# Message-passing kernel on 100,000 nodes: places of the search as rows, index loads cut in pieces, dense units moved, scatter turns refined

## What is computed

```python
x = normal(100000, 128)                       # nodes
src = randint(25000); dst = sort(100000 * uniform(25000)**2)   # edges, sorted by dst
# layer 0: edge messages, maximum over the edges of one destination
xc = x[dst];  feat = concat([xc, x[src] - xc])
m  = relu(feat @ W1 + b1) @ W2 + b2
a  = segment_max(m, dst);  a[no edge] = 0
x1 = layernorm(x + a)
# layer 1: sum of the sources' rows, then two products, with a residual
h  = x1 + segment_sum(x1[src], dst)
h  = relu(h @ V1 + c1) @ V2 + c2
out = layernorm(x1 + x1 @ Wres + bres + h)
```

## Time and profile before

| what | value |
|---|---|
| time, median of 3 runs | 1157.18 us (1156.98 to 1157.43) |
| profiled execution, its own time | 1157.41 us |
| its span | 1155.6 us, so 1.81 us lie around it |
| busy in the span | PE 1083.7 us (94%), DVE 939.1 (81%), ACT 896.5 (78%), POOL 764.7 (66%) |
| stages, from start times in the trace | head to 57.5, S to about 278, A to about 588, dense units to 605.8, B to about 925, C to 1136.3, scatters to 1155.6 |

### The profile page before, as it was taken

How to read it: one execution, slowest core, us unless ns; L and a number is a source line. 1 busy time by engine, 2 the same in 40 slices (tenths; PEclk the granted TensorE clock), 3 DMA queues, 4 the chain that set the end, 5 groups by cost and what they waited for, 6 DMA issues and landing times.

```text
span 1155.6 us, 27075 instructions
## 1 busy us (share of the span) xinstructions
PE 1083.7 (94%) x7463; PEld 836.6 (72%) x7463; DVE 939.1 (81%) x3648; ACT 896.5 (78%) x3876; POOL 764.7 (66%) x798
## 2 busy tenths in 40 slices
PE   4699999999999999999979999999999999999992
PEld 3477777776666666666658888888888888888882
DVE  5588988987888888888858778777777799999981
ACT  1578888887888888888867888888888877777772
POOL 6777777777777766662037777777777777777006
PEclk9899999999999999999989999999999999999997
DMA  4578778885787887776566666666655566666532
GB/s 135 173 225 233 238 238 242 240 235 169 196 223 216 219 231 204 216 216 181 169 196 199 211 204 191 210 206 191 206 173 180 182 217 220 215 217 221 180 135 82
DMA packets 172193, 232.04 MB, mean 201 GB/s; under 512 B 25508, under 2 KB 90641, under 8 KB 172044
## 3 DMA queue, kind: packets, MB, share of 16 engines
q1 hardware_dynamic: 145372, 180.84, 49.9%
q0 software_dynamic: 25088, 48.94, 16.8%
q10 hardware_dynamic: 1584, 0.53, 0.2%
HBM read 129.48 MB, written 102.96 MB: 201 GB/s over the span
## 4 chain that ended last, share of the span: by engine, by line
PE 54%; POOL 26%; issue 10%; DVE 7%; DMA 1%; ACT 1%; DVEq 0%; SPq 0%; POOLq 0%; ACTq 0%
POOL edge_rows L507 16%; PE psY L1100 10%; PE psY L1099 10%; PE psH L1108 9%; PE psT L1092 5%; POOL xd_early L507 4%; PE psE L1092 4%; POOL src_bc L507 4%; PE psE L1100 4%; PE psE L1099 4%; PE psE L1251 4%; PE psE L1215 3%; DVE shared L733 3%; DVE shared L744 2%; POOL out L511 1%
## 5 line engine op out<-in xcount | busy, mean ns | idle before, releaser
L1099 PE MATMUL psY<-wc,hT 128*128 128x128 f32 x1568 | 305.9, 277 | 2.6 <-ACT o_rows L948 2.2
L1100 PE MATMUL psY<-wcr,xT 128*128 128x128 f32 x1568 | 305.3, 277 | 0.0
L511 POOL DMA_INDIRECT out<-edge_rows,idx x196 | 195.0, 995 | 116.7 <-DMA out<-o_rows 57.5
L507 POOL DMA_INDIRECT edge_rows<-x1e_table,idx x196 | 189.0, 965 | 124.6 <-DMA x1e_table<-shared 65.1
L923 ACT ACTIVATE junk<-psY 128x128 f32<-128x128 f32 x784 | 209.5, 300 | 50.9 <-PE psY L1100 50.9
L1099 PEld LDWEIGHTS psY<-wc,hT 128*128 128x128 f32 x1568 | 240.7, 194 | 3.9 <-issue 3.9
L1100 PEld LDWEIGHTS psY<-wcr,xT 128*128 128x128 f32 x1568 | 240.4, 194 | 0.0
L507 POOL DMA_INDIRECT edge_rows<-in_x,idx x196 | 190.2, 970 | 66.0 <-issue 59.5
L585 DVE TENSOR_SCALAR x<-x_in,mv,rs 128x128 f32<-128x128 f32 x784 | 220.5, 359 | 0.5
L1108 PE MATMUL psH<-xT,wc 128*128 128x512 f32 x392 | 205.5, 606 | 16.0 <-DVE deltas L664 10.2
L579 DVE BATCH_NORM_STATS2 bn_a<-x_in 128x6 f32<-128x128 f32 x784 | 164.6, 271 | 19.6 <-DMA x_in<-in_x 19.5
(11 more groups left out here) (125 smaller groups left out, 1996.3 us busy)
## 6 DMA issues: line engine op xcount, KB each, us to landing
x_in<-in_x SPq DMA_DIRECT2D x196, 256.0 KB
out<-o_rows SPq DMA_DIRECT2D x196, 256.0 KB
src_bc<-src_dram SPq DMA_DIRECT2D x49, 256.0 KB, 4.9
mask<-mask_dram SPq DMA_DIRECT2D x98, 128.0 KB
x1eT_spill<-x1eT SPq DMA_DIRECT2D x49, 256.0 KB, 2.5
x1e_table<-edge_rows SPq DMA_DIRECT2D x49, 256.0 KB, 3.3
x1e_table<-shared SPq DMA_DIRECT2D x49, 256.0 KB, 3.7
x1eT<-x1eT_spill SPq DMA_DIRECT2D x49, 256.0 KB, 3.1
```

The source lines that it names most:

```text
L507: nc.gpsimd.indirect_dma_start(to, None, table, bass.IndirectOffsetOnAxis(idx[:, what, t:t + 1], 0)).then_inc(landed[n % FLIGHT], 16)
L511: nc.gpsimd.indirect_dma_start(table, bass.IndirectOffsetOnAxis(idx[:, SCAT, t:t + 1], 0), frm, None, bounds_check=limit, oob_is_err=False ...
L1099: t_.matmul(to[:, cut(t)], h[:, cut(t)], wc2[:, :], start=t == 0, stop=False, skip_group_check=True)
L1100: last = t_.matmul(to[:, cut(t)], xt[:, cut(t)], wcr[:, :], start=False, stop=t == TILES - 1, skip_group_check=True)
```

## The change

1. `place` writes its results as rows. One stationary window of 128 columns out of `place_w` is zero except for two columns, at 2g and 2g+1. Three products with the 512 columns of `match` and `steps` as the moving operand add the group's pair of rows to `psE[2]`, where all 49 groups accumulate. `keep_places` is gone from the steps. `lead_a` copies the bank, PE transposes it in four tiles, and DVE copies the pairs out.
2. Index loads of 67 rows become 64 and 3, those of 127 rows 112 and 15, also the copy of `parts`. One more small load reads the last destinations of three tiles. In all 8 more DMAs from SP, all in the head.
3. Head: the scaling of unit 1 on DVE moves ahead of a wait for PE, and PE waits for the second weights only before it first uses them.
4. Steps 49, 50 and 51 of A now each end with a whole dense unit. Four dense units still follow. B starts at unit 79 in place of 76, and C has 3 units fewer.
5. Scatter turns: groups 45, 46, 47 have turns of their own, and so have the first three tiles of group 48; only its last tile waits for all stores. The last unit stores only the 160 rows that are its own, without the wait.

```diff
+    A_LAST = FIRST_A + A_UNITS
+    BORDER = A_LAST + STEPS - GROUPS
+    EVEN = 16
+    PART_ROWS = (FULL - P) // EVEN * EVEN
+    PAIR_AT = 2 * GROUPS - 2
+    WINDOW = PAIR_AT + P
...
-            for s in range(STEPS):
+            for s in range(GROUPS):
                 step_a(s, FIRST_A + s // A_STEPS if s // A_STEPS < A_UNITS else None, s % A_STEPS)
+            for s in range(GROUPS, STEPS):
+                step_a(s, None, 0)
+                dense(A_LAST + s - GROUPS)
...
-                    if n == UNITS - 1:
-                        sp.wait_ge(stored[(n - 1) % SLOTS], 16 * ((n - 1) // SLOTS + 1))
-                    sp.dma_start(rows_of(out, n), o_rows[:, n % SLOTS, :]).then_inc(stored[n % SLOTS], 16)
+                    own = slice((UNITS * ROWS - N) // TILES if n == UNITS - 1 else 0, P)
+                    sp.dma_start(rows_of(out, n)[own, :], o_rows[own, n % SLOTS, :]).then_inc(stored[n % SLOTS], 16)
...
-                sp.dma_start(parts_above[1:P, :, :], parts[0:P - 1, :, :]).then_inc(s_above, 16)
+                sp.dma_start(parts_above[EVEN:P, :, :], parts[EVEN - 1:P - 1, :, :]).then_inc(s_above, 16)
+                sp.dma_start(parts_above[1:EVEN, :, :], parts[0:EVEN - 1, :, :]).then_inc(s_above, 16)
...
+            def load_second(to, a, done):
+                rows = a.rearrange("(j p) -> j p", p=P)
+                sp.dma_start(to[0:PART_ROWS, :], rows[0:PART_ROWS, :]).then_inc(done, 16)
+                sp.dma_start(to[PART_ROWS:FULL - P, :], rows[PART_ROWS:FULL - P, :]).then_inc(done, 16)
...
+            for g in range(WHOLE):
                 pool.wait_ge(res_done, g + 1)
+                if g % SLOTS == 0 or g > LATE:
+                    await_stores(count)
...
+            for g in range(WHOLE, GROUPS):
+                pool.wait_ge(res_done, g + 1)
+                for t in range(TILES):
+                    await_stores(count if t < WHOLE_TILES else 16 * BODIES)
+                    if t + 1 < WHOLE_TILES:
+                        count = stores_needed(WHOLE + t + 1)
                     scatter(out, edge_rows[:, cut(g * TILES + t)], g * TILES + t, scatter_number(g) + t)
...
             def lead_a():
-                dve.wait_ge(places_done, GROUPS)
+                dve.wait_ge(pos_done, GROUPS)
+                v.tensor_copy(place_rows, psE[2][:, :]).then_inc(rows_kept, 1)
+                copy_xs(0)
+                dve.wait_ge(rows_turned, 1)
+                v.tensor_copy(places.rearrange("p (g t) c -> p t g c", t=TILES),
+                              tiles(psE[3][:, :])[:, :, 0:2 * GROUPS]
+                              .rearrange("p t (g c) -> p t g c", c=2)).then_inc(places_done, 1)
...
-                    for t in range(TILES):
-                        to = psE[2 + q][:, 2 * t:2 * t + 2]
-                        t_.matmul(to, match[:, q, cut(t)], place_w[:, 0:2], start=True, stop=False,
-                                  skip_group_check=True)
-                        t_.matmul(to, steps[:, r, 0, cut(t)], place_w[:, 2:4], start=False, stop=False,
-                                  skip_group_check=True)
-                        last = t_.matmul(to, steps[:, r, 1, cut(t)], place_w[:, 2:4], start=False, stop=True,
-                                         skip_group_check=True)
+                    t_.matmul(psE[2][:, :], place_w[:, 0, window], match[:, q, :], start=g == 0, stop=False,
+                              skip_group_check=True)
+                    for h in range(2):
+                        last = t_.matmul(psE[2][:, :], place_w[:, 1, window], steps[:, r, h, :], start=False,
+                                         stop=g == GROUPS - 1 and h == 1, skip_group_check=True)
...
             def lead_a():
                 pe.wait_ge(match_done, GROUPS)
-                pe.wait_ge(places_done, GROUPS)
                 transpose_in(0)
+                pe.wait_ge(rows_kept, 1)
+                transpose4(psE[3], place_rows, rows_turned)
...
                 if n > 0:
-                    dense(n)
+                    first_half(n)
+                if n == 2:
+                    pe.wait_ge(s_dv, WEIGHT_STEPS)
+                second_product(n - 2)
...
             link(v.tensor_tensor(wtmp[:, 0, :], raw[:, RES, :], ident[:, :], ALU.add))
+            norm1_scale(1)
             dve.wait_ge(s_pe, 2)
...
-            pe.wait_ge(s_dv, WEIGHT_STEPS)
             walk(head, dense, lead_s, step_s, lead_a, step_a, lead_b, step_b)
```

More of the change, by code:

```diff
@@ L28, in gnn_program @@
     BODIES = UNITS // SLOTS
-    assert UNITS == BODIES * SLOTS and N % 32 == 0
+    assert UNITS == BODIES * SLOTS and N % 32 == 0 and (UNITS * ROWS - N) % TILES == 0
     GROUPS = -(-E // ROWS)
@@ L98, in gnn_program @@
         assert WHOLE % SLOTS == 0
-        last_dst = sb("last_dst", [1, WHOLE], I32)
-        stores_16 = sb("stores_16", [1, WHOLE], I32)
+        WHOLE_TILES = FULL - WHOLE * TILES
+        LATE = WHOLE - SLOTS
+        last_dst = sb("last_dst", [1, WHOLE + WHOLE_TILES], I32)
+        stores_16 = sb("stores_16", [1, WHOLE + WHOLE_TILES], I32)
         x_in = sb("x_in", [P, SLOTS, ROWS])
@@ L176, in gnn_program @@
         pos_done = sem("pos_done")
+        rows_kept = sem("place_rows_kept")
+        rows_turned = sem("place_rows_turned")
         places_done = sem("places_done")
@@ L539, in _, with stores_needed, await_stores, last_group_of @@
                     gather(edge_rows[:, cut(g * TILES + t)], x1e_table, PLACE, g * TILES + t, z_number(g) + t)
-            def stores_needed(g):
-                top = g + SLOTS - 1
-                earlier = pool.value_load(stores_16[0:1, top:top + 1], min_val=0, max_val=16 * LAST)
+            def stores_needed(at):
+                earlier = pool.value_load(stores_16[0:1, at:at + 1], min_val=0, max_val=16 * LAST)
                 return pool.snap(earlier + 16)
+            def await_stores(count):
+                for k in range(SLOTS):
+                    pool.wait_ge(stored[k], count)
+                pool.nop().then_inc(s_turn, 1)
+            def last_group_of(g):
+                return g + SLOTS - 1 if g < LATE else g
             pool.wait_ge(s_dv, SETUP_STEPS)
-            count = stores_needed(0)
-            for g in range(GROUPS):
-                r = g % SLOTS
+            count = stores_needed(last_group_of(0))
+            for g in range(WHOLE):
                 pool.wait_ge(res_done, g + 1)
-                if g < WHOLE and r == 0:
-                    for k in range(SLOTS):
-                        pool.wait_ge(stored[k], count)
-                    pool.nop().then_inc(s_turn, 1)
-                elif g == WHOLE:
-                    for k in range(SLOTS):
-                        pool.wait_ge(stored[k], 16 * BODIES)
-                for t in range(TILES):
-                    if t == TILES - 1 and r == SLOTS - 1 and g + 1 < WHOLE:
-                        count = stores_needed(g + 1)
+                if g % SLOTS == 0 or g > LATE:
+                    await_stores(count)
+                for t in range(TILES):
+                    if t == TILES - 1 and (g % SLOTS == SLOTS - 1 or g >= LATE):
+                        count = stores_needed(last_group_of(g + 1) if g + 1 < WHOLE else WHOLE)
+                    scatter(out, edge_rows[:, cut(g * TILES + t)], g * TILES + t, scatter_number(g) + t)
+            for g in range(WHOLE, GROUPS):
[4 more added lines that the diff above has]
+                        count = stores_needed(WHOLE + t + 1)
                     scatter(out, edge_rows[:, cut(g * TILES + t)], g * TILES + t, scatter_number(g) + t)
@@ L626, in dense @@
             def dense(n):
-                norm1_scale(n + 1)
+                if n > 0:
+                    norm1_scale(n + 1)
                 norm1_var(n + 2)
@@ L652, in find @@
                                     ALU.is_equal).then_inc(match_done, 1)
-            def keep_places(g):
-                if is_group(g):
-                    dve.wait_ge(pos_done, g + 1)
-                    v.tensor_copy(places[:, g * TILES:(g + 1) * TILES, :],
-                                  psE[2 + g % 2][:, 0:2 * TILES]
-                                  .rearrange("p (n c) -> p n c", c=2)).then_inc(places_done, 1)
             def lead_s():
-                dve.wait_ge(s_above, 32)
+                dve.wait_ge(s_above, 48)
                 v.tensor_tensor(deltas[:, :, :, :].rearrange("p a h j -> p a (h j)"), parts, parts_above,
```

46 lines of the change are left out of this document (26 added, 20 removed).

## The result

The changed kernel takes **1144.44 us** (median of 4 runs, 1143.42 to 1146.15) against 1157.31 (1156.98 to 1157.93) for the one before: ratio 0.989, interval 0.9873 to 0.9907. The prediction was 1144.5. The profiled execution of the changed kernel is the longest of its four: 1146.15 us, span 1144.0. Its ledger therefore closes at -11.6 us of span, where the medians differ by 12.9.

What follows compares the result with a forecast made beforehand. PE was taken to bound S and C, with holes in the head and at A's end, and POOL scattering after PE's last product. Terms +16.9, +0.3, -14.5, -4.4, -11.2 sum to -12.9: 1157.41 to 1144.5 us, range 1138.5 to 1152.0.

Steps and rivals of the forecast that it cites:

- places in S: Search stage S: three wide products at 0.645 us replace twelve at 0.30; step 4.25 us grows by 0.345, +16.9 us.
- `lead_a`: Start of A: added copies and four transposes mostly fit PE's 0.77 us wait for ACT; +0.3 us, between 0 and 2.5.
- head: Before S: smaller row counts shorten SP's issues and PE's 10.2 us hole goes; net -14.5 us, between -17.5 and -9.
- units at the end of A: A's end to B: three more dense units fill PE's idle time, paced by ACT; -4.4 us, between -1 and -9.
- turns and tail: Span's end: finer turns let POOL scatter earlier, span ending at 1144.4; -11.2 us, between -10.5 and -12.
- what was named as late next: End of head: the first sources' broadcast, sent near 41, needing 4.9 us; PE waits 1 us, then 2.2 for a `finish`.
- B's first step near 613: Sign for the units at A's end: B's first step starts near 613 us.
- The counts 12, 5 and 3: Last twenty scatters: twelve go early, five at 1128.4, three wait for the last store.
- (d): Rival in S: wide products overlap down to the narrow ones' price, S stays as before; 1127.6 us, chance 0.03.
- (e): Rival in the head: number of DMAs binds SP, not rows; hole stays, head +2.3, 1161.3 us; chance 0.05.
- (b): Rival in the head: another transfer takes the hole's place, 6 to 9 us remain; head -7, 1152 us, chance 0.17.
- (c): Rival: full cover at A's end and the head at its best, 5 to 6 us more; 1138.5 us, chance 0.11.

Runs made afterwards that it cites:

- run 1: The changed kernel measured again with no edit: 1144.77 us, ratio 0.9902 to the kernel before.
- run 2: The changed kernel with the twelve narrow products, the copies in each step and the old `lead_a` back: 1128.34 us, ratio 0.9754 to the kernel before.
- run 3: The kernel before with the wide products and new `lead_a`, plus the extra load of last destinations and the last short store without its wait: 1173.3 us, ratio 1.0126.
- run 4: The changed kernel with index loads of 67 and 127 rows whole again, the copy of `parts` still cut: 1150.92 us, ratio 0.9948 to the kernel before.
- run 5: The changed kernel with the copy of `parts` cut into 113 and 14 rows instead of 112 and 15: 1151.28 us, ratio 0.9953 to the kernel before.
- run 6: The changed kernel with the head's old order (unit 1 scaled after DVE's waits, PE waiting for all weights first): 1145.94 us, ratio 0.9889 to the kernel before.
- run 8: The changed kernel with the three dense units moved from the end of A back to C: 1149.67 us, ratio 0.9944 to the kernel before.
- run 9: The changed kernel with the old scatter turns, one for four groups and one for the last group: 1155.49 us, ratio 0.9986 to the kernel before.
- run 10: The changed kernel with the last group's counts read before its first wait: 1144.49 us, ratio 0.9897 to the kernel before.

## Why the prediction was right

The ledger, from starts in the traces. "After" is the execution whose own time is 1146.15, "again" is run 1. For S the predicted 0.345 times 49 is kept, as 38 steps give 0.346 each.

| term | predicted | after | again |
|---|---|---|---|
| places in S | +16.9 | +16.9 | +16.9 |
| `lead_a` | +0.3 | -0.2 | -0.2 |
| head | -14.5 | -13.2 | -14.5 |
| units at the end of A | -4.4 | -4.8 | -5.0 |
| turns and tail | -11.2 | -10.4 | -10.9 |
| sum, with A +0.1 | -12.9 | -11.6 | -13.6 |

- **Places.** Right: 0.65 us for three, a step of 4.59. The value was chosen by the distance between starts of the same form; that was the choice that mattered. By the Trainium skill's 131 ns the step would be an estimated 4.34, and the forecast 12 us too low. Runs 2 and 3 price the part at 16.4 and 15.1 to 15.7, net of `lead_a` and of when S began.
- **`lead_a`.** Taken at +0.3 and found at -0.2. From the last `candidates` to A's first product it is 13.21 us against 12.69, of which two places are 0.69. The copies and transpositions hid behind the wait of the earlier trace rows, and nothing was late behind them.
- **Head.** The mechanism held, by runs 4 and 5, and so did what was named as late next: PE waits 1.83 and 1.09 us for the broadcast and its consequences, with 1 and 2.2 predicted, in the other order of size. Within the sum there were errors that cancel. The load of unit 4 went out at 13.84, not near 12: an issue for 64, 15 or 3 rows costs 0.44 to 0.59, not the 0.29 taken for each. The broadcast needed 6.3 us from its issue (39.79) until DVE could go on (46.12), 6.5 in run 1, not the median of 4.9. The second wait was for ACT's copy of `xT`, not for a `finish`. The order of unit 1 gave nothing (run 6). The first `candidates` came at 47.2 rather than 49, but the unit behind it waited, so that only the later ones give the gain of the head. In profiles of the same head (runs 1, 8, 9 and 10, and run 6 with its old order) the eleventh `candidates` starts between 93.96 and 94.82, in "after" at 95.54: a head of -13.9 to -14.8 is the usual, and -13.2 the run with the lower clock.
- **Units.** Right in size: from A's last step B comes 4.4 us later than before, with three units more done and 4.9 predicted. The sign "B's first step near 613" is met as well: 605.8 plus 2.7 plus 4.9 is 613.4, and the step starts at 613.84. One wait of 1.55 us is left of the load's 5.02, as said. What the sum had only in passing is the clock, 1.00 in place of 0.90; that ACT paces the units fits the profile but stays argued.
- **Turns.** The counts 12, 5 and 3 were right. The 2.29 us for the store were misread: by the earlier trace rows it had landed after 2.04, and the scatter at 1136.17 merely kept its place in the row of 1.29. From the scaling's end to the landing it is 2.29 in "after" by luck, 1.82 in run 1, 1.78 to 1.86 in six other profiles and 2.11 in run 6. Mis-sized was also "0.35 for reading the count": from landing to scatter there are 1.46 us, 0.5 of them the reads and 0.9 what run 10 leaves. The 0.3 each for waits between the scatters was not there: 1.29 and 1.28. So the tail is 16.1 to 16.6 and not 15.8.
- **Rivals.** (d) fell by runs 2 and 3. (e) fell by runs 4 and 5. (b) and (c) each had a grain: a transfer does take the hole's place, at 3 us instead of 6 to 9, and the end of A is slightly better than its term.

The forecast met the median to 0.1 us. That much is luck: its terms were off by up to 1.3 us each with both signs, and the same kernel varies by 2.7 us. What it had right is the mechanism of each part, and its size to within that 1.3 us.

## What to carry to other kernels

Fewer instructions are not cheaper on a bound PE: price a product by the distance between starts in a stream, per moving column, and a form that streams 512 columns three times loses to one that streams 2 columns twelve times; 16 us were lost by that inside a change that gained 13. When a DMA issue takes microseconds, look at the row counts of the transfers ahead of it before counting bytes or pieces. When a hole in the bound engine closes, name the transfer that is late next and expect a gain there to be taken back by its neighbour in the same queue.

## What the runs showed of the hardware

- One row decides: behind a copy of 113 rows SP's next issue takes 3.87 us and PE stands 8.24; behind one of 112 rows it is 1.88 and 0.32.
- A matmul of 2 columns with a stationary operand of its own starts every 0.025 us, loads included, beside 0.215 for 512 columns; 0.215 also held in an accumulation over 49 steps into one bank.
- With the same two waits of PE (1.85 and 1.09 us), one execution went on at a granted clock of 1.00 and another at 0.74 for 6.5 us, and took 1.66 us more for the unit. The same at the end of A: behind waits of 1.67 and 1.32 us the clock stayed at 1.00 (run 1) or fell to 0.50 for 5.5 us (run 6), which cost 1.7. Differences of this size between single profiles of this kernel say nothing of an edit.
- On POOL, 0.92 us lie between the landing that a turn waits for and the next DMA, of which the profile leaves 0.54 unexplained; reading the count adds 0.5.
